# Two routing stages: raw rows stored during attention, picks in two parts, one-hot sums of row ids only

## The reference

```
x  = x + attention(layernorm(x), adj)                 # both layers
xn = layernorm(x)
# layer 0: the gate and the experts see xn
p  = softmax(xn @ gate_w + gate_b); top-2 of p -> (val1, e1), (val2, e2)
x  = x + sum_k val_k * (gelu(xn @ W1[e_k] + b1[e_k]) @ W2[e_k] + b2[e_k])      # H = 512
# layer 1: the gate sees xn; the experts see xe[e] = layernorm(xn) * ln_g[e] + ln_b[e]; w = p_top / p_top.sum()
x  = x + sum_k w_k * (gelu(xe[e_k] @ W1[e_k] + b1[e_k]) @ W2[e_k] + b2[e_k])   # H = 1024
```

## Time and profile before

| | us |
|---|---|
| median of three runs | 1789.14 |
| profiled execution | 1787.74 |
| its span | 1786.0 |
| layer 0: routing, last logit to `slot_w` | 444.9 to 481.4 |
| layer 0: expert tiles | 481.4 to about 720 |
| layer 1: routing, last logit to `slot_w` | 1304.2 to 1342.4 |
| layer 1: expert tiles | 1342.4 to 1786 |

### The profile page before, as it was taken

The page is one execution under the profiler, slowest core; times in us unless marked ns, Lnnn a source line. Parts: engine busy times, 40 slices in busy tenths (PEclk is TensorE's granted clock), DMA queues, the critical chain, the costliest instruction groups (busy, mean ns, idle before and its releaser), DMA issues.

```text
span 1786.0 us, 41369 instructions
## 1 busy us (share of the span) xinstructions
PE 1660.1 (93%) x13364; PEld 1535.9 (86%) x13365; DVE 931.6 (52%) x2186; ACT 955.8 (54%) x2194; POOL 351.8 (20%) x314
## 2 busy tenths in 40 slices
PE   4799999999799999589999999999988999999998
PEld 3588888878789999479999999999978999999997
DVE  4578868778612222568888878877780111111111
ACT  1143444435334433368989989899743444444443
POOL 2110000000156666320000000000002333333332
PEclk9899999999899999799999999999999999999999
DMA  9990000003478887400000000000375666666664
GB/s 160 108 176 10 10 10 9 28 28 125 143 190 208 229 209 186 159 10 18 14 14 19 9 19 18 10 19 14 110 281 175 176 177 179 182 186 186 176 176 97
DMA packets 86495, 189.98 MB, mean 106 GB/s; under 512 B 13737, under 2 KB 60585, under 8 KB 77577
## 3 DMA queue, kind: packets, MB, share of 16 engines
q1 hardware_dynamic: 53705, 139.39, 23.5%
q0 software_dynamic: 31360, 48.45, 17.2%
q10 hardware_dynamic: 1344, 1.05, 0.2%
HBM read 188.98 MB, written 33.11 MB: 124 GB/s over the span
## 4 chain that ended last, share of the span: by engine, by line
PE 52%; DVE 3%; ACT 1%; issue 1%; DMA 1%; DVEq 0%; POOL 0%; ACTq 0%; POOLq 0%
PE bank L1774 24%; PE bank L2285 12%; PE bank L2324 11%; PE bank L707 1%; PE bank L710 1%; PE bank L2292 1%; ACT arena L1476 1%; DVE arena L1612 0%; PE bank L2173 0%; PE bank L697 0%; DVE arena L1610 0%; DMA arena<-xe 0%; DVE X L2107 0%; PE bank L2180 0%; PE bank L2165 0%
## 5 line engine op out<-in xcount | busy, mean ns | idle before, releaser
L1774 PE MATMUL bank<-arena 128*128 128x195 bf16 x5408 | 467.1, 248 | 14.2 <-DVE arena L1612 10.9
L1774 PEld LDWEIGHTS bank<-arena 128*128 128x128 fp8e4 x5408 | 463.8, 97 | 17.6 <-issue 16.7
L1476 ACT ACTIVATE arena<-arena,m_row 128x512 fp8e5<-128x512 f32 (+1 forms) x672 | 401.5, 678 | 44.5 <-DVE arena L1612 32.8
L2285 PEld LDWEIGHTS bank<-X,arena 128*128 128x128 f32 x2832 | 337.1, 194 | 8.7 <-issue 2.3
L2388 DVE TENSOR_TENSOR arena<-bank,X 128x256 f32<-128x256 f32 x118 | 50.1, 425 | 563.7 <-PE bank L2324 563.7
L2285 PE MATMUL bank<-X,arena 128*128 128x128 f32 x2832 | 339.2, 277 | 0.1
L2324 PE MATMUL bank<-arena,X 128*128 x1416 | 325.2, 379 | 2.5 <-ACT X L2362 2.0
L1319 PE MATMUL bank<-arena 128*128 (+1 forms) x1352 | 312.1, 386 | 15.1 <-DVE arena L1225 15.1
L1319 PEld LDWEIGHTS bank<-arena 128*128 128x128 f32 x1352 | 252.5, 191 | 55.7 <-issue 20.9
L2324 PEld LDWEIGHTS bank<-arena,X 128*128 128x128 f32 x1416 | 259.9, 190 | 33.7 <-issue 3.1
L2362 ACT ACTIVATE X<-bank,arena 128x128 f32<-128x128 f32 x708 | 196.0, 379 | 70.2 <-issue 61.5
(11 more groups left out here) (249 smaller groups left out, 1346.2 us busy)
## 6 DMA issues: line engine op xcount, KB each, us to landing
arena<-m1w SPq DMA_DIRECT2D x67, 1024.0 KB, 10.6
arena<-m0w SPq DMA_DIRECT2D x67, 512.0 KB, 7.1
xs<-X SPq DMA_DIRECT2D x4, 1664.0 KB, 7.1
arena<-qd SPq DMA_DIRECT2D x25, 256.0 KB, 3.1
arena<-adjT POOLq DMA_DIRECT2D x13, 448.0 KB, 12.9
arena<-adjT POOLq DMA_DIRECT2D x13, 384.0 KB, 10.8
xe<-zeros POOLq DMA_DIRECT2D x1, 3456.0 KB, 21.7
X<-x_in SPq DMA_DIRECT2D x2, 1664.0 KB, 11.5
```

Of the source, the lines that this page charges most:

```text
L1476: last = a.activation(self.sign[slot].bitcast(F8W)[:, q * W:q * W + nt * P], self.row[r][:, 0:nt * P], ACT.Sigmoid, scale=STEEP, bias=self ...
L1774: last = pe.matmul(bank[rb * NT + n][:, kind * KW:(kind + 1) * KW], self.split[slot][kind].bitcast(F8)[:, q * W + n * P:q * W + (n + 1) * ...
L2285: last = pe.matmul(bank[2 * s + c // 4][:, c % 4 * P:(c % 4 + 1) * P], self.W1[s][:, k * HID + c * P:k * HID + (c + 1) * P], self.rxt[s][: ...
```

## The change

- **Rows.** `X` is not normalised in place any more. The raw rows go to `xs` while they become final: in layer 0 pair by pair beside the store to `xd`, in layer 1 in three pieces beside the store to `out`. A row of `xs` has four more columns (1040 bytes): scale, shift, first weight, second weight minus first weight. These 26 x 4 columns of each partition are stored when the weights are known, by one DMA of 3328 pieces of 16 bytes, and the gathers wait for it. After a gather, VectorE normalises the gathered tile (`norm`), three tiles ahead, and TensorE's transpose waits for that.
- **Picks.** Logits of tiles 0 to 19 go to bank 2, those of 20 to 25 to bank 7. VectorE picks for the first 20 tiles when their logits are there, then for the last six.
- **One-hot operands.** Only ids are summed (59 columns). Second picks add 4096 to the id; at the end the sum is split into the id and a 0 or 1, and `norm` makes the weight of a slot from it. ScalarE writes 10 of the 13 products of a part, VectorE three. The weights are made in part 1, and the tile table after part 3.
- Filler products: 20 and 88 in place of 48 and 96.

The diff, cut to its core:

```diff
-                    for a, b, final in ((0, T - 2, 6), (T - 2, T, 7)):
+                    for a, b, final in ((0, 12, 3), (12, 24, 6), (24, T, 7)):
                         sp.wait_ge(rows_final, final)
+                        sp.dma_start(xs[a * P:b * P, 0:D]..., X[:, a * D:b * D]...).then_inc(self.rows_stored, 16)
                         sp.dma_start(total[a * P:b * P, :]..., X[:, a * D:b * D]...).then_inc(self.x_spilled, 16)
...
-                load_w2(range(4))
-                for g in range(2):
-                    sp.wait_ge(self.x_scaled, (g + 1) * PAIRS)
-                    sp.dma_start(xs[g * PAIRS * P:(g + 1) * PAIRS * P, :]..., X[...]...).then_inc(self.xn_stored[g], 16)
-                load_w2(range(4, 8))
+                for g in range(8):
+                    sp.dma_start(self.W2[:, g * n:(g + 1) * n], ...).then_inc(self.w2_loaded, 16)
+                sp.wait_ge(self.weights_ready, 1)
+                sp.dma_start(xs[0:NP, D:ROW].rearrange("(t p) c -> p t c", p=P), self.row_cols
+                             ).then_inc(self.cols_stored, 16)
...
-                with v.Fori(0, PAIRS) as i:
-                    for s in range(2):
-                        ...
-                        v.tensor_scalar(xv, xv, self.scale_x[:, at(t, 1)], self.shift_x[:, at(t, 1)],
-                                        ALU.mult, ALU.add).then_inc(self.x_scaled, 1)
...
+                for (a, b), logits_bank in zip(PICK_PARTS, (bank[2], bank[7])):    # (0, 20), (20, 26)
+                    pick_part(a, b, logits_bank)
...
                 for c in range(4):
...
-                    if c == 0:
+                    if c == 1:
                         weights()
...
-                    v.tensor_tensor(tiles_[:, :, 0, :], eq, over(ids, G), ALU.mult).then_inc(self.hot_ids[b], 1)
-                    if c == 1:
-                        tile_table()
+                    v.tensor_tensor(self.hot_tile[b][:, 0:few * G]..., eq[:, 0:few, :], over(ids[...], G), ALU.mult
+                                    ).then_inc(self.hot_ids[b], 1)
+                tile_table()
...
-                v.tensor_copy(slot_w[:, :], bank[5][:, G:2 * G]).then_inc(self.slots_ready, 1)
+                step(v.tensor_scalar(slot_w[:, :], slots, float(SECOND), None, ALU.is_ge))
+                step(v.tensor_scalar(self.spare, slots, 0.0, spare_row[:, :], ALU.is_equal, ALU.mult))
+                step(v.scalar_tensor_tensor(out=self.spare, in0=slot_w[:, :], scalar=-float(SECOND), in1=self.spare, ...))
+                v.scalar_tensor_tensor(out=slot_row[:, :], in0=slots, scalar=1.0, in1=self.spare, ...)
...
-                    for q in range(PAIRS):
+                    for q in range(IDS_ON_DVE, PAIRS):                                 # ScalarE: 10 of 13
...
-                pool.wait_ge(self.slots_ready, 2)
-                for s in range(2):
-                    pool.wait_ge(self.xn_stored[s], 16)
+                pool.wait_ge(self.slots_ready, 1)
+                pool.wait_ge(self.rows_stored, self.n_stored)
+                pool.wait_ge(self.cols_stored, 16)
                 for g in range(4):
                     gather(g)
...
-                        pe.wait_ge(self.rx_loaded[(q + 2) % 4], 16 * (j + 1 + (q >= 2)))
+                        pe.wait_ge(self.rx_ready, g + 3)
                         turn_x((q + 2) % 4)
...
+                def norm(g, s, nth):
+                    x = self.rx[s]
+                    v.wait_ge(self.rx_loaded[s], 16 * nth)
+                    v.scalar_tensor_tensor(out=slot_w[:, at(g, 1)], in0=slot_w[:, at(g, 1)], scalar=x[:, D + 3:D + 4],
+                                           in1=x[:, D + 2:D + 3], op0=ALU.mult, op1=ALU.add)
+                    v.tensor_scalar(x[:, 0:D], x[:, 0:D], x[:, D:D + 1], x[:, D + 1:D + 2], ALU.mult, ALU.add
+                                    ).then_inc(self.rx_ready, 1)
...
+                    if not isinstance(g, int) or g + 3 < RUN_TILES:
+                        norm(g + 3, (q + 3) % 4, j + 1 + (q >= 1))
```

More of the change, by code:

```diff
@@ L1925, in __init__ @@
                 self.places_ready = sem(tag + "places_ready")
-                self.xn_stored = [sem(f"{tag}xn_stored{s}") for s in range(2)]
+                self.rows_stored = sem(tag + "rows_stored")
+                self.n_stored = (3 if second_norm else PAIRS) * 16
+                self.cols_stored = sem(tag + "cols_stored")
                 self.ysum_ready = sem(tag + "ysum_ready")
@@ L2011, in route_vector @@
+                v.scalar_tensor_tensor(out=shift, in0=mv[:, 0:T], scalar=-1.0, in1=scale, op0=ALU.mult, op1=ALU.mult)
+                v.tensor_scalar(self.second_id, row_id[:, :], float(SECOND), None, ALU.add
+                                ).then_inc(self.second_ids, 1)
                 TE = T * E
-                lg3 = self.logits.rearrange("p (t e) -> p t e", e=E)
                 w3 = self.work.rearrange("p (t e) -> p t e", e=E)
-                def spread(a):
-                    return a.rearrange("p (t o) -> p t o", o=1).to_broadcast([P, T, E])
@@ L2017, in spread_t @@
[L2017 to L2027, removed]
-                    step(v.tensor_tensor(w3, w3, spread_t(order8[:, :]), ALU.mult))
-                    step(v.tensor_reduce(self.best, w3, AXX, ALU.max))
-                    step(v.tensor_tensor(p3, w3, spread(self.best), ALU.is_equal))
-                    if top is self.top1:
-                        step(v.tensor_tensor(w3, lg3, spread(top), ALU.subtract))
-                        v.tensor_copy(self.shares, self.work).then_inc(self.picked, 1)
-                        step(v.scalar_tensor_tensor(out=self.logits, in0=pick, scalar=-3.0e38, in1=self.logits,
-                                                    op0=ALU.mult, op1=ALU.add))
@@ L2377, in tiles_vector, with tile @@
             def tiles_vector(self, v):
+                def norm(g, s, nth):
[5 more added lines that the diff above has]
+                                    ).then_inc(self.rx_ready, 1)
+                v.wait_ge(self.slots_ready, 1)
+                for g in range(3):
+                    norm(g, g, 1)
                 v.wait_ge(self.tiles_known, 1)
-                v.wait_ge(self.slots_ready, 2)
                 v.wait_ge(self.b_loaded, 32)
-                def tile(i, s):
-                    g = 2 * i + s
+                def tile(j, q):
+                    g, i, s = 4 * j + q, 2 * j + q // 2, q % 2
                     e = v.value_load(expert_of[0:1, at(g, 1)], min_val=0, max_val=E - 1)
@@ L2392, in tile @@
                                     ).then_inc(self.ry_ready[s], 1)
-                for s in range(2):
-                    tile(0, s)
-                with v.Fori(1, RUN_TILES // 2) as i:
-                    for s in range(2):
-                        tile(i, s)
-                tile(RUN_TILES // 2, 0)
+                    if not isinstance(g, int) or g + 3 < RUN_TILES:
+                        norm(g + 3, (q + 3) % 4, j + 1 + (q >= 1))
+                for q in range(4):
+                    tile(0, q)
+                with v.Fori(1, RUN_TILES // 4) as j:
+                    for q in range(4):
+                        tile(j, q)
+                for q in range(3):
+                    tile(RUN_TILES // 4, q)
         def all_stats(v, stat):
```

168 lines of the change are left out of this document (98 added, 70 removed).

## The result

The change makes the kernel slower: 1827.98 us (median of 4 runs, 1821.58 to 1833.86) against 1788.75 us of the kernel before (4 runs), a ratio of 1.0217, 95% interval 1.0181 to 1.0252. The prediction was 1777, and the range ended at 1800. The profiled execution after spans 1827.1 us, 41.1 more than before.

The account below looks back on a forecast made before the run. TensorE's product chain was taken to bound the kernel, touched where it passes through VectorE's routing. Terms -6.9 - 8.2 + 1.2 + 2.0 = -11.9 gave 1775.8 from the profiled 1787.74, set at 1777; range 1768 to 1800.

Parts of the forecast that it names:

- The loop of layer 0: Normalising ends 0 to 0.1 us after TensorE wants the tile, for each of 56 tiles; taken as 2 us lost.
- The rival for this loop: Layer 0's tile loop: normalising 0.25 us late through a register step or wait; 55 tiles lose 14 us, 1789 to 1791; chance 0.08.
- the sign of transposes "without idle time ahead of them": In layer 0's tile loop, TensorE's transposes without idle time before them would show the forecast right.
- the other sign, the period: Layer 0's tile loop: 3.73 us a tile would show the forecast right, near 4.0 the rival about late normalising.
- The lists: Routing's slot lists ready at 474.5 in layer 0 and 1334.2 in layer 1, 6.9 and 8.2 us sooner.
- The "half" rival: One-hot parts stay near 20 us because TensorE's clock falls in a gap or part 2 waits; about 1783 us, chance 0.08.
- the narrower products: One-hot parts: TensorE's 26 products with half the columns take 3.0 us a part, between 1.6 and 3.13.
- W1 and the first norm: Before each layer's first transpose: one normalising adds 0.6 us a layer, 1.2 in all; W1's later release adds nothing.
- It costs nothing by itself: Routing: the tile table, which releases W1, moves behind part 3, where VectorE waits for TensorE anyway; no cost.
- The 16-byte store: The first gather of each layer waits for it; landing takes 8 to 15 us, hidden or 2 us late.
- the first rival: First gather of each layer: the small-piece store decides; at 26 us landing, +14 us, 1803; chance 0.20.
- The picks: Routing, picking in two parts: ends at 449.3 in layer 0, 2.0 us sooner, and 1308.7 in layer 1, 4.9 sooner.

Follow-up runs that it names:

- the read ahead: Changed kernel with TensorE's register read of the tile's expert moved to the head of the tile, before the wait for the normalised row: 1789.95 us, 0.9974 of the kernel before.
- table back: Changed kernel with that register read moved and one-hot products on 118 columns, plus the tile table again behind the second one-hot part: 0.9948 of the kernel before.
- the kernel with 118 columns and the read ahead: Changed kernel with the register read at the tile's head and one-hot products 118 columns wide as before: 1782.88 us, 0.9931 of the kernel before; run again 0.9957.

## Why the prediction was wrong

**The loop of layer 0: the failed step.** The prediction set the end of the norm against the moment at which "TensorE wants the tile for its transpose", found "0 to 0.1 us for each of 56 tiles, up to 6 us", and took 2. That comparison is right: the transposes started in time, and with the read ahead 55 turns of the loop take 212.8 to 213.2 us from transpose to transpose, against 208.8 before, 4.0 to 4.4 more. It asked only for the instruction that waits, not for what is queued behind it on TensorE: that term was put at nothing. There the register read stood; before, it ran while the first product was still running, and behind a wait that ends on the last moment it is added in full: 0.7 us x 56, some 39 us. The rival for this loop named a register step, but priced it at 0.25 us and gave it 0.08. And the sign of transposes "without idle time ahead of them" did not show the fault, since they had none; the other sign, the period, did, with 4.58 for 3.73.

**The lists: right in size, given back by the clock.** With the clock at 1.0 the lists came 6.6 and 8.4 us sooner; forecast were 6.9 and 8.2. In the changed kernel itself it was 2.7 and 1.2. The "half" rival had the clock, but put its fall into a gap; the runs put it into the narrower products, which the prediction had counted as cost-free at 3.0 us a part.

**W1 and the first norm: under-priced.** From the list to the first product the prediction added 1.2 us over both layers; with the lists early it is 1.5 + 4.2. The norm itself is not far off: with W1 out of the way the first transposes came 0.7 and 0.9 us later behind the list than before (*table back*), forecast 0.6 each. "It costs nothing by itself" was right for VectorE and wrong for the DMA engines: a table made later sends W1 into the gathers.

**The 16-byte store: hidden, as forecast,** and the first rival wrong. It landed in 5.7 to 6.0 us, under the estimate of 8 to 15. The rule of the Trainium skill (DMA: Bandwidth & Descriptors, Specifications) that had been taken as a price per piece does not show here at 26 us. The picks came within 0.3 us in both layers; 16 steps at 0.35 are 5.6 us, not 5.5 as added up for layer 0, which changes nothing.

Put together with what was measured, the sum of the prediction is the kernel with 118 columns and the read ahead: it was 0.9931 and 0.9957 of before, -12.4 and -7.7 us, against the -11.9 of the sum. That the first comes so near is in part luck: by the table the lists give -15.0 as forecast, but the way to the first product costs 5.7, not 1.2, and the stretch with the loop 1.0, not 2.0, which adds up to -8.3. Both were faster than the kernel before and the changed kernel, so what the change is about works; its loss is the place of one read, and a part of its gain went with the narrower products.

## What to carry to other kernels

When a change makes a wait late, go down the waiting engine's own program: whatever is not engine work behind that wait, register reads above all, comes on top of it, once per turn of the loop; read registers ahead of the wait. When a result that the engine waits for hangs on the engine's own last product, write the ring down and add it up, since each small step in it then counts in full. And a transfer that is released later starts against other transfers: ask what it meets there.

## What the runs showed of the hardware

- A register read held TensorE's sequencer for 0.65 to 0.70 us, of which the load took 0.30, and two took twice that. The timeline shows it only as "issue" ahead of the next product; the view of its source line shows its steps.
- One-hot products on 59 and on 118 columns take the same 0.12 us at full clock, but the granted clock fell to 0.50 within 9 of 10 stretches of the narrow ones, and did not fall in any of 12 of the wide in the same order of work.
- 3328 pieces of 16 bytes landed 5.5 to 6.8 us after their issue, less than 2304 pieces of 4 bytes, for which the queue waited 16.8 us.
- Two loads of 1 MB sent out 2.7 us ahead of the first gathers held these up by 3.5 us; sent out 11.8 us ahead they did not.
